# Expert loop of a gated attention block: weight addresses from a table, and 128-column matmuls throughout

## What is computed

```python
def reference(x, ctx_768, ...):            # x (4, 1024, 256), ctx (4, 77, 192)
    x = x + tanh(g_xattn) * cross_attention(layernorm(x), ctx_768)
    x = x + tanh(g_ffn) * ffn(layernorm(x))

def ffn(x):                                # D 256, H 1024, E 8 experts, top 2
    gate_weights = softmax(x @ gate_w + gate_b)
    topk_values, topk_indices = top_k(gate_weights, 2)
    hidden = relu(einsum('bsd,edh->bseh', x, w1) + b1)
    expert_out = einsum('bseh,ehd->bsed', hidden, w2) + b2
    sel = take_along_axis(expert_out, topk_indices[..., None], axis=2)
    return sum(topk_values[..., None] * sel, axis=2)
```

## Time and profile before

| | us |
|---|---|
| median of 3 runs | 792.27 (792.18 to 792.4) |
| the profiled execution | 793.41 |
| its span, first to last instruction | 791.1 |
| PE busy | 633.0 (80%) |
| ACT, DVE, POOL busy | 423.2, 413.6, 235.7 |
| tile loop, first row load on PE to last matmul | about 306 to 777 |

### The profile page before, as it was taken

The page is one execution under the profiler, slowest core; times in us unless marked ns, Lnnn a source line. Parts: engine busy times, 40 slices in busy tenths (PEclk is TensorE's granted clock), DMA queues, the critical chain, the costliest instruction groups (busy, mean ns, idle before and its releaser), DMA issues.

```text
span 791.1 us, 19049 instructions
## 1 busy us (share of the span) xinstructions
PE 633.0 (80%) x4937; PEld 513.6 (65%) x4937; DVE 413.6 (52%) x1163; ACT 423.2 (54%) x1073; POOL 235.7 (30%) x269
## 2 busy tenths in 40 slices
PE   1967547617738454989999999999999999999992
PEld 1455445516527353678888788888888888888882
DVE  2044764783783683854455455555555545444451
ACT  0235245244252442556666666666666666666661
POOL 2000154134214402336664222222222222222221
PEclk9965555555555556989999999999999999999997
DMA  7300441243244203223322322222322222222211
GB/s 224 126 0 35 173 155 61 100 160 141 89 159 162 108 1 122 49 57 79 69 43 43 44 44 45 44 44 45 46 40 46 43 43 43 43 42 43 43 22 20
DMA packets 40205, 57.28 MB, mean 72 GB/s; under 512 B 6583, under 2 KB 34733, under 8 KB 38959
## 3 DMA queue, kind: packets, MB, share of 16 engines
q1 hardware_dynamic: 26047, 37.52, 15.2%
q0 software_dynamic: 14064, 18.55, 13.7%
HBM read 33.19 MB, written 24.49 MB: 73 GB/s over the span
## 4 chain that ended last, share of the span: by engine, by line
PE 55%; DVE 2%; issue 2%; DMA 1%; ACT 1%; DVEq 0%; POOL 0%; SPq 0%; ACTq 0%; POOLq 0%
PE hid L1315 10%; PE bank L1330 10%; PE hid L1311 8%; PE bank L1331 7%; PE bank L1332 7%; PE hid L1314 6%; PE hid L1312 4%; PE bank L1296 2%; DMA pool<-xs 0%; DMA out_dram<-pool,idx 0%; DVE pool L1062 0%; ACT pool L700 0%; DVE pool L1083 0%; DVE pool L1075 0%; POOL out_dram L564 0%
## 5 line engine op out<-in xcount | busy, mean ns | idle before, releaser
L564 POOL DMA_INDIRECT out_dram<-pool,idx x71 | 111.4, 1570 | 306.6 <-ACT pool L707 248.9
L1062 DVE TENSOR_TENSOR pool<-hid,pool 128x512 f32<-128x512 f32 x142 | 97.9, 691 | 159.7 <-ACT pool L691 153.4
L691 ACT ACTIVATE pool<-hid,b1s 128x128 f32<-128x128 f32 x568 | 165.1, 373 | 24.9 <-PE hid L1315 22.6
L1330 PE MATMUL bank<-w2h,pool 128*128 x568 | 155.2, 273 | 4.4 <-issue 2.3
L1311 PE MATMUL hid<-pool,w1h 128*128 128x256 f16 x568 | 156.1, 275 | 0.6 <-DVE pool L1062 0.6
L1315 PE MATMUL hid<-pool,w1h 128*128 128x256 f16 x568 | 155.7, 274 | 0.1
L1332 PE MATMUL bank<-w2h,pool 128*128 x568 | 154.6, 272 | 0.0
L1331 PE MATMUL bank<-w2l,pool 128*128 x568 | 154.6, 272 | 0.0
L1312 PE MATMUL hid<-pool,w1l 128*128 128x128 f16 x568 | 124.9, 220 | 0.0
L1314 PE MATMUL hid<-pool,w1l 128*128 128x128 f16 x568 | 124.8, 220 | 0.0
L700 ACT ACTIVATE pool<-pool 128x512 f16<-128x512 f32 x142 | 89.4, 630 | 22.9 <-DVE pool L1062 22.9
(11 more groups left out here) (212 smaller groups left out, 894.6 us busy)
## 6 DMA issues: line engine op xcount, KB each, us to landing
pool<-in_L_ffn_w_dram SPq DMA_DIRECT2D x16, 1024.0 KB, 7.3
pool<-xs SPq DMA_DIRECT2D x71, 132.5 KB
xb<-in_x_dram SPq DMA_DIRECT2D x4, 1024.0 KB, 9.6
out_dram<-xb SPq DMA_DIRECT2D x4, 1024.0 KB, 3.9
out_dram<-pool,idx POOLq DMA_INDIRECT x71
xs<-xext,dest POOLq DMA_INDIRECT x64
pool<-in_L_ffn_b_dram SPq DMA_DIRECT2D x1, 1024.0 KB, 5.0
w1h<-in_L_xattn_Wq_dram SPq DMA_DIRECT2D x1, 256.0 KB, 5.1
```

The costliest lines, as they stand in the source:

```text
L564: g.indirect_dma_start(out=out_rows, out_offset=bass.IndirectOffsetOnAxis(ap=idx[s % U][:, 0:1], axis=0), in_=y2[s % 3], in_offset=None, c ...
L691: a.activation(hb[:, c * P:(c + 1) * P], bank[c // 2][:, (2 * (c % 2) + 1) * P:2 * (c % 2 + 1) * P], ACT.Identity, bias=b1s[:, ds(e * NH + ...
L1062: v.tensor_tensor(part, main, part, ALU.add).then_inc(g_hb, 1)
L1330: t.matmul(o, hh[s % 2][:, hs], wh, start=c == 0, stop=False)
```

## The change

PE no longer adds a base to each address. POOL writes a table `adr` once, of 48 addresses per expert (two w1 parts for each of 16 (c, dc), and two w2 parts for each of 8 c), by four iotas into partition 0 of `VO`, which the attention has finished with. Each entry is the final SBUF address, so `part_at` holds the byte positions of the four weight tensors. `base_tab` becomes `at_tab`: expert times 48, the place of the expert's row in the table. PE loads that one word per tile (`load_at`) and then the addresses, 16 registers by one load (`load_adr`), three times per tile: twice in `output(s)` (c = 3 and 5) for the w1 parts of tile s + 2, once in the middle of `hidden(s)` for the w2 parts of tile s - 1.

In `hidden`, a pair of w1 parts takes three 128-column matmuls into one 128-column result: high with x high, high with x low, low with x high. A tile has 48 such matmuls in place of 32, and its result takes two PSUM banks in place of four. `h_bias` is gone from ACT; DVE adds the bias itself, from the PSUM bank and a broadcast of `b1s`, in two operations of 512 columns.

```diff
-    NHB = NH // 2
+    NHB = NH // 4
+    NA = 4 * NH + 2 * NH
+    W0 = 16512
+    part_bytes = 2 * E * ND * H
+    part_at = [W0 + k * part_bytes + (2 * (P - 1) if k < 2 else 0) for k in range(4)]
...
+        adr = VO[0:1, 0:E * NA].bitcast(I32).rearrange("p (e n) -> p e n", e=E)
...
+            pool.wait_ge(s_x1, B * T)
+            for k in range(2):
+                g.iota(adr[:, :, 0:4 * NH].rearrange("p e (c d k) -> p e c d k", d=ND, k=2)[:, :, :, :, k],
+                       [[2 * ND * H, E], [2 * P, NH], [2 * H, ND]], base=part_at[k],
+                       channel_multiplier=0).then_inc(s_adr, 1)
+                g.iota(adr[:, :, 4 * NH:NA].rearrange("p e (c k) -> p e c k", k=2)[:, :, :, k],
+                       [[2 * NH * D, E], [2 * D, NH]], base=part_at[2 + k],
+                       channel_multiplier=0).then_inc(s_adr, 1)
             pool.wait_ge(s_outd, B * 16)
...
-            def h_bias(s):
-                act.wait_ge(s_tab, 3 * (round_of(s) + 1))
-                e = act.value_load(exp_tab[0:1, s:s + 1], min_val=0, max_val=E - 1)
-                for c in range(NH):
-                    if c % 2 == 0:
-                        act.wait_ge(g_mm1, NHB * s + c // 2 + 1)
-                    if s and c % (NH // 2) == 0:
-                        act.wait_ge(g_hl, 2 * s - 1 + 2 * c // NH)
-                    a.activation(hb[:, c * P:(c + 1) * P], bank[c // 2][:, (2 * (c % 2) + 1) * P:2 * (c % 2 + 1) * P],
-                                 ACT.Identity, bias=b1s[:, ds(e * NH + c, 1)]).then_inc(g_tb, 1)
...
-                v.tensor_scalar(base_tab[:, at], exp_tab[:, at], 2 * ND * H, None, ALU.mult).then_inc(s_tab, 2)
+                v.tensor_scalar(at_tab[:, at], exp_tab[:, at], NA, None, ALU.mult).then_inc(s_tab, 2)
...
-            def h_parts(s):
+            def h_parts(s, e):
                 for j in range(2):
-                    dve.wait_ge(g_tb, NH * s + (j + 1) * NH // 2)
-                    main = hid[:, j * H:(j + 1) * H].rearrange("p (c k t) -> p c k t", k=2, t=P)[:, :, 0, :]
-                    part = hb[:, j * H // 2:(j + 1) * H // 2].rearrange("p (c t) -> p c t", t=P)
-                    v.tensor_tensor(part, main, part, ALU.add).then_inc(g_hb, 1)
+                    dve.wait_ge(g_mm1, NHB * s + j + 1)
+                    if s:
+                        dve.wait_ge(g_hl, 2 * s - 1 + j)
+                    half = slice(j * H // 2, (j + 1) * H // 2)
+                    v.tensor_tensor(hb[:, half].rearrange("p (c t) -> p c t", t=P), bank[j].rearrange("p (c t) -> p c t", t=P),
+                                    b1s[:, ds(e * NH + j * NH // 2, NH // 2)].rearrange("p (c a) -> p c a", a=1).to_broadcast(
+                                        [P, NH // 2, P]), ALU.add).then_inc(g_hb, 1)
...
+            def load_at(s):
+                pe.wait_ge(s_tab, 3 * (round_of(s) + 1))
+                reg = pe.alloc_register(f"at{s}")
+                pe.reg_load(reg, at_tab[0:1, s:s + 1])
+                at_row[s] = pe.snap(reg, donate=True, min_val=0, max_val=(E - 1) * NA)
+
+            def load_adr(s, first):
+                regs = [pe.alloc_register(f"adr{s}_{first + n}") for n in range(2 * NH)]
+                pe.reg_load(regs, adr.rearrange("p e n -> p (e n)")[:, ds(at_row[s] + first, 2 * NH)])
+                for n, r in enumerate(regs):
+                    adr_of[s, first + n] = r
+
+            def part(k, s, n):
+                lo = part_at[k]
+                size = 2 * P if k < 2 else 2 * D
+                val = pe.snap(adr_of[s, n], donate=True, min_val=lo, max_val=lo + part_bytes - size,
+                              guaranteed_mod_val=lo % size, out_of_modulus=size)
+                return w_b[k][:, ds(val - lo, size)].bitcast(F16)
...
                         pe.wait_ge(g_hb, 2 * s - 1 + 2 * c // NH)
-                    o = bank[c // 2][:, (c % 2) * 2 * P:(c % 2 + 1) * 2 * P]
+                    if c == NH // 2 and s >= 1:
+                        load_adr(s - 1, 4 * NH)
+                    o = bank[2 * c // NH][:, c % 4 * P:(c % 4 + 1) * P]
                     for dc in range(ND):
-                        wh, wl = (part(w, s, dc * H + c * P, P) for w in (w1h_b, w1l_b))
-                        xhl, xh = xt[:, 2 * dc * P:2 * (dc + 1) * P], xt[:, 2 * dc * P:(2 * dc + 1) * P]
-                        if dc == 0:
-                            t.matmul(o, wh, xhl, start=True, stop=False)
-                            t.matmul(o[:, 0:P], wl, xh, start=False, stop=False)
-                        else:
-                            t.matmul(o[:, 0:P], wl, xh, start=False, stop=False)
-                            mm = t.matmul(o, wh, xhl, start=False, stop=True)
-                    if c % 2:
+                        wh, wl = (part(k, s, (c * ND + dc) * 2 + k) for k in range(2))
+                        xh, xl = (xt[:, (2 * dc + k) * P:(2 * dc + k + 1) * P] for k in range(2))
+                        t.matmul(o, wh, xh, start=dc == 0, stop=False)
+                        t.matmul(o, wh, xl, start=False, stop=False)
+                        mm = t.matmul(o, wl, xh, start=False, stop=dc == ND - 1)
+                    if c % 4 == 3:
                         mm.then_inc(g_mm1, 1)
...
-                    if c == 2 and s + 2 < S:
-                        load_base(s + 2)
-                    wh, wl = (part(w, s, c * D, D) for w in (w2h_b, w2l_b))
+                    if s + 2 < S:
+                        if c == 1:
+                            load_at(s + 2)
+                        if c == 3:
+                            load_adr(s + 2, 0)
+                        if c == 5:
+                            load_adr(s + 2, 2 * NH)
+                    wh, wl = (part(2 + k, s, 4 * NH + 2 * c + k) for k in range(2))
```

More of the change, by code:

```diff
@@ L89, in gated_attention_and_routed_experts @@
         row_tab = sb("row_tab", [1, S], I32)
-        base_tab = sb("base_tab", [1, S], I32)
+        at_tab = sb("at_tab", [1, S], I32)
         exp_tab = sb("exp_tab", [1, S], I32)
@@ L241, in gated_attention_and_routed_experts @@
         s_posl = sem("s_posl")
+        s_adr = sem("s_adr")
         s_padc = sem("s_padc")
@@ L344, in gated_attention_and_routed_experts @@
         g_mm1 = sem("g_mm1")
-        g_tb = sem("g_tb")
         g_hb = sem("g_hb")
@@ L710, in _ @@
             rows_T(1)
-            h_bias(0)
             h_hi(0)
@@ L716, in _ @@
                 if s + 1 < S:
-                    h_bias(s + 1)
                     h_hi(s + 1)
@@ L1080, in _ @@
             gate(1, e[1])
-            h_parts(0)
+            h_parts(0, e[0])
             dve.wait_ge(s_b2, 16)
@@ L1090, in _ @@
                 if s + 1 < S:
-                    h_parts(s + 1)
+                    h_parts(s + 1, e[s + 1])
                 y_sum(s, e[s])
@@ L1272, in _ @@
                 batch(b)
[L1274 to L1286, removed]
+            w_b = [w[:].bitcast(U8) for w in (w1h, w1l, w2h, w2l)]
+            at_row = {}
+            adr_of = {}
+            def load_at(s):
[14 more added lines that the diff above has]
+                return w_b[k][:, ds(val - lo, size)].bitcast(F16)
             def turn_rows(s):
@@ L1337, in _ @@
             pe.wait_ge(s_posl, 1)
-            load_base(0)
-            load_base(1)
+            pe.wait_ge(s_adr, 4)
+            load_at(0)
+            load_adr(0, 0)
+            load_adr(0, 2 * NH)
             turn_rows(0)
@@ L1342, in _ @@
             hidden(0)
+            load_at(1)
+            load_adr(1, 0)
+            load_adr(1, 2 * NH)
             for s in range(S):
@@ L1347, in _ @@
                     hidden(s + 1)
+                else:
+                    load_adr(s, 4 * NH)
                 output(s)
```

## The result

The changed kernel takes 799.66 us (median of 4, 798.35 to 800.0), the kernel before 792.22 (792.05 to 792.4) on the same chip: a ratio of 1.0091 with a 95% interval of 1.0073 to 1.0108. It is 0.9% slower, where 731 us had been forecast, with a range of its own of 724 to 745. The profiled execution took 798.35 us, with a span of 796.3. This is rival (b), loads partly serial, on its slower side.

What follows compares the result with a forecast made beforehand. PE's sequencer, with its address additions, was taken to cost 0.99 us per tile; (6.47 - 5.53) x 64 = 60.2 us from the loop plus 1.4 around it, 61.6 off 792.3, gave 731 us, range 724 to 745.

Steps and rivals of the forecast that it cites:

- rival (b): PE's register loads partly serial, 0.9 to 1.5 us each: 745 to 860 us; chance 0.10, half of it faster.
- 3 L - 2.47: Exposed us per tile from three 16-register loads of L us each, once L exceeds what queued pairs hide in both stages.
- point of no gain: Load length at which exposed time eats the whole 0.94 us gain per tile: L = 1.14 us.
- The additions: PE's sequencer: 48 addresses less one formed per tile by additions, about 0.11 us each with its pair; these should vanish.
- The pitch of 128-column pairs: Hidden stage: 48 weight-load and matmul pairs 0.056 us apart, 2.69 us a tile against 2.64 before.
- rival (c): Long runs of 128-column pairs slower than 0.056 us; at 0.098, 7.72 us a tile and 872 us; chance 0.06.
- The lead of 16 pairs: PE's sequencer runs 16 pairs ahead, hiding 0.89 us of load in the hidden stage, 1.75 in the output stage.
- Loads in the output stage: Two w1 loads, 2 x (L + 0.11), against 1.37 us lead plus 0.65 between: nothing exposed up to L = 0.90.
- The bias and the ends: Outside the steady loop: bias on DVE wins 1.5 us at early tiles, 0.4 at the end; setup costs 0.5.
- (d): Scatter or row chain binds once tiles are shorter: at 5.9 us a tile, 755 us; chance 0.05.
- (e): Addresses still need an addition each on PE: 7.3 us a tile, 848 us; chance 0.03.
- Rival (a): Each word of PE's three loads is its own trip: 5.0 us a load, 18.1 a tile, 1535 us; chance 0.20.

Runs made afterwards that it cites:

- e5: Changed kernel with eight more register loads ahead of tile 0, of 32, 24, 12, 8, 4, 2, 16 and 1 words; 807.23 us, one run.
- e9: Changed kernel with eight more register loads ahead of tile 0, of 1 to 13 words, one of them from the table's third word; 803.28 us, one run.
- e2: Changed kernel with the 48 addresses loaded once ahead of tile 0, so every tile uses one expert's weights (result not the reference's); 727.98 us.
- e8: Kernel before with table, loads of 16 and old wide matmuls, its output-stage loads at blocks 3 and 5 as in the change; 755.62 us.
- e3: Changed kernel with its second load of w1 addresses moved from column block 5 of the output stage to block 7; 758.3 us.
- e1: Changed kernel with loads of 16 registers removed and additions back; 128-column matmuls, two PSUM banks and bias on DVE stay; 790.08 us.
- e4: Kernel before with only the table and loads of 16 added, at output blocks 2 and 6 and mid hidden stage; 733.05 us.

## Why the prediction was wrong

*The step that failed* is one term: "I take a value near the lower end, 0.3 to 0.8" for a load of 16 registers. It measured 1.106 us, and 1.36 in the median at the place where it meets the beginning of a scatter's transfer, for which the prediction had no term. The bounds, 0.31 to 5.0, held it. The choice between them didn't: "one instruction with one source row" was read as the price of one word, and a load of 16 costs four steps of about 0.26 (e5, e9). The nearest row was one of a single word, and a row with one word can't tell a price per instruction from one per word or per group.

*The formula around it held.* The prediction had the exposed time of a tile as 3 L - 2.47 and the point of no gain at L = 1.14. With the three loads at their medians, 1.106 + 1.36 + 1.106 = 3.57, it gives 1.10 exposed and 5.53 + 1.10 = 6.63 us a tile; 6.59 was measured. In part that is luck: by its own terms the hidden load would stand out by 1.106 + 0.22 - 0.89 = 0.44 and the two of the output stage by 0.67, where the waits are 0.27 and 0.85 a tile. The mean load, 1.19, lies just beyond the point of no gain, and so does the result. Rival (b) had been given only 0.10, with this very condition, and slower as a whole 0.31. The time lies within the wide range of 724 to 830, on the side of the kernel before that was thought the less likely.

*The additions* (0.99 us a tile lost to the sequencer): right. They are gone, and e2 reaches 5.52.

*The pitch of 128-column pairs*: right at 0.056, through 48 in a row, so rival (c) is out. The Trainium skill ("TensorE: Matmul & The Clock Gate", Back-to-back issue gap), which puts such a stream at 81 ns each, doesn't agree with these traces: 0.056 us is measured, and the measurement decides.

*The lead of 16 pairs*, read from the earlier trace rows: right, and it decided. In the kernel after 13 to 14 weight loads start while a load of 1.106 us runs, and 15 to 16 with the register instruction ahead of it. During the second w1 load only 5 start there, and 8 at the same place in e8. The Trainium skill (same page, Architectural detail, queue depths) gives 64 entries, 32 pairs. An estimate from that, 32 x 0.056 = 1.79 us, would have covered the hidden load, and it stood out by 0.31. The prediction's point of no gain for such a queue, 1.65 us, comes out at about 1.73 by its own terms, which changes nothing here.

*Loads in the output stage*: the prediction pooled the two loads and the pairs between them, which hides where the loss is: the first is free, the second pays about 0.86 us. Two blocks later it costs 13.8 / 62 = 0.22 (e3).

*The bias and the ends*: right in size. By tile 6 the kernel was 1.3 us ahead where 1.5 - 0.5 = 1.0 was taken, at the end about 1.0 where 0.4 was taken, and e1, which has the bias on VectorE at an unchanged pace, is 1.7 us faster where 1.5 + 0.4 was taken. How much of it is the bias the runs don't separate. (d) and (e) are out by e2.

*Rival (a)*, every word a trip of its own, is wrong for aligned groups of four and right for what lies outside them. The Trainium skill ("Runtime: NRT & Kernel Launch", Instruction fetch mechanics) has about 200 ns a register even in bulk; the page speaks of register loads from HBM, and these come from on-chip memory. An estimate by that is 3.2 us for 16 words; they take 1.106, but 2 and 3 words (0.547, 0.782) come near it.

## What to carry to other kernels

A register load is hidden only by the matmuls already queued when it starts, here 15 to 16 pairs at most and fewer shortly behind another load, so each load is to be held against the *time* of those pairs, not its sum against the tile: wider matmuls, loads far apart, and two short loads in place of a long one all recover what the additions had cost. If the trace has a load of one word only, measure the size you mean to use before you choose between one trip and many. Of the versions run here the best changes the least: the table and the loads of 16 with the old matmul shapes, 733.05 us against 791.69.

## What the runs showed of the hardware

- The length of a register load from on-chip memory goes by steps: 0.31 to 0.33 us for the first, 0.23 to 0.27 for each further one. A group of four words that starts at a multiple of four shares a step; words left over or out of step (one load of four from the third word, 1.000) take one each. So 4 words (0.333) are cheaper than 2 (0.547), and 16 (1.106) cost no more than 13 (1.099).
- A load of 16 that is under way when an indirect scatter's transfer begins takes up to 0.35 us longer (1.458 against 1.107). One that starts half a microsecond or more after its first packet isn't longer (37 loads of e4 of 1.102 to 1.113, with 74 packets or more under each).
- The addresses in registers cost nothing that shows: 128-column weight loads were 0.056 us apart with each address in a register of its own, where one addition each had made it 0.11.
